# An attention layer and an FP4 feed-forward layer: weight squares in PSUM, rests of x on VectorE, attention up to three batches ahead

## The chip, the cores and the metric

The kernel runs on one core of one Trainium2 chip. The metric is the device time of one execution in microseconds (us), the median of several runs.

## The reference

`out` is x with 8 batches of T = 512 rows and D = 256 columns. An attention-like layer without softmax comes first, then a feed-forward layer whose linear maps quantise both operands to FP4 in blocks of 16:

```python
v = out @ W_write.T                                  # values
S = out[t] . out[s-1]; M = gamma**(t-1-s), s < t     # scores, decayed and causal
x = layernorm(out + out + alpha * ((S * M) @ v) @ W_read.T)
def fp4(x):                                          # blocks of 16 along the last axis
    scale = max(max(abs(block)) / 6, 1e-12)
    return nearest_of(0, .5, 1, 1.5, 2, 3, 4, 6)(abs(block) / scale) * sign(block) * scale
h = silu(fp4(x) @ fp4(w_gate).T) * (fp4(x) @ fp4(w_up).T)    # 704 columns
x = layernorm(x + fp4(h) @ fp4(w_down).T)
```

## The kernel before, in words

**Precision.** Every matmul is done as three: each operand is split into a rounded part (`_hi`, type fp32r, by ScalarE) and a rest (`_lo`, the difference, by VectorE or GpSimd), and hi*hi, hi*lo and lo*hi are added up in PSUM. `split_matmuls` issues the three terms one after the other for each slice of the contraction (its lines 1526, 1527 and 1528 are the three terms in the profile). Everything that feeds it therefore has three steps: filled, rounded (`xT_hi_ready` and so on), rest (`xT_lo_ready`).

**Weights.** The six parts of w_ffn (4 for gate and up, 2 for down, 128 x 704 each) go through the FP4 quantiser once: `w_maxima`, `w_divisors`, `w_reciprocals` (VectorE), `w_normalise` (GpSimd), `w_squares` (ScalarE), `w_magic_add` and `w_to_grid` (VectorE), `w_dequant` (GpSimd). Nine fills then transpose them: `w_transpose` and `w_subtract` (TensorE), `w_round` and `w_remainder` (ScalarE). `combine` multiplies the two attention weights into `comb`, scaled by `scale_comb` and split by `round_comb` and `rest_comb`.

**Attention of batch n.** `x_round` (ScalarE) and `x_rest` (GpSimd) split the transposed x, of which there is one buffer (`x_full`, `xT_hi`, `xT_lo`); `scores(n, j)` for 4 row tiles of 512, 384, 256 and 128 columns; `decay_scores` (VectorE, writes `pr`), `p_round`, `p_rest`; `values(n, u)`, `v_round`, `v_rest`; `reads(n, u)`; `x_residual` (z), `x_deviations`, `x_moments`, `x_rstd`, `x_layernorm` (writes `x1`, two buffers, by which batches' attention may be ahead of the feed-forward layer); then the FP4 quantiser of x (`x_maxima` to `x_dequant`), `xq_transpose`, `xq_round`, `xq_rest`.

**Feed-forward of tile k** (32 tiles of 128 rows, k = 4b + t): `gate_up(k, b, t, half)`, `gate_silu`, `hidden`, the quantiser of h (`h_maxima` to `h_dequant`), `h_repeat`, `h_transpose(k, t, g)`, `h_round`, `h_rest`, `down(k, t)`, `out_residual`, `out_deviations`, `out_moments`, `out_rstd`, `out_layernorm`, `store`.

**What sets the order.** Each of the five engine blocks (and SP's list of loads and stores) is an order written out by hand: a head, a `body(b, par)` that `run` repeats for b = 2 to 5, and a tail. An engine does its list strictly in order; each helper waits on semaphores for its inputs and for the buffers that it overwrites (`wait_ge`), and a `free` list names what frees a PSUM bank. PSUM has 8 banks: four of `gu` for gate_up, and `bank[0]` to `bank[3]`, shared by all else by the tables `v_bank`, `s_bank`, `r_bank`, `h_bank`, `d_bank`, `w_bank`. TensorE starts with 28 matmuls on zeros.

Of the kernel before, what the change touches and what calls it, by code (L numbers as in the profile page):

```python
# [30 lines left out]
F32 = mybir.dt.float32  # L31
# [6 lines left out]
P = 128  # L38
# [14 lines left out]
def mk_seq_postln_kernel(nc, x_rows, xt_rows, w_attn, w_ffn, decay, log_alpha, out):  # L53
# [12 lines left out]
    WU = 6  # L66
    LAST = B - 1
    p_at = [sum(T - P * i for i in range(j)) for j in range(TILES + 1)]

    with ExitStack() as ctx:  # L70
# [47 lines left out]
        x1 = sb("x1", [P, 2, TILES, D])  # L118
# [32 lines left out]
        o_off = sb("o_off", [P, 2, D])  # L151
# [13 lines left out]
        w_bank = (bank[0], gu[:, 3, :], bank[0], gu[:, 2, :], gu[:, 1, :], gu[:, 0, :], bank[2], bank[2], bank[0])  # L165
# [43 lines left out]

        def w_dst(w):  # L210
            return wq_gu[:, w * I:(w + 1) * I] if w < 4 else wq_dn[:, w - 4, 0:I]
# [23 lines left out]
        def run(body):  # L235

            for b in range(2, B - 2):
                body(b, b % 2)
# [5 lines left out]
        def _(sp):  # L244
# [81 lines left out]
        def _(pool):  # L326
# [1534 lines left out]
```

## Time and profile before

| | |
|---|---|
| median of 3 runs (lowest, highest) | 336.72 us (336.69, 338.21) |
| profiled execution, its own time | 336.96 us |
| its span in the trace | 335.2 us |
| TensorE matmul busy | 319.0 us, 95%, 2271 instructions |
| VectorE busy | 293.7 us, 88%, 750 |
| GpSimd busy | 250.6 us, 75%, 261 |
| ScalarE busy | 213.4 us, 64%, 516 |
| TensorE on the chain that ended last | 75% |

In the profile PE is TensorE, PEld its weight loads (they overlap the matmuls), DVE is VectorE, ACT is ScalarE, POOL is GpSimd, SP issues DMAs. Matmuls overlap, so their rate is read from start to start, not from the length of one. The granted clock is a share of 2.4 GHz; the other level is 1.2 GHz, 0.50.

### The profile page before, as it was taken

The page shows a single profiled execution, that of the slowest core. Times are in us where ns is not written, and L with a number is a line of the kernel's source. Part 1 is how long each engine was busy: PE and PEld are TensorE (multiplying, and loading weights), DVE is VectorE, ACT ScalarE, POOL GpSimd, SP SyncE. Part 2 cuts the span into 40 slices and gives each one's busy share as a digit, 9 for nine tenths or more (in the row PEclk, how much of TensorE's full clock was granted, in tenths as well). Part 3 has the DMA queues.
Part 4 walks back from the last instruction along what each step waited for, and adds up shares of the span by engine and source line. Part 5 has one row for each costly group of instructions (what it writes and reads, how often), then busy time and mean ns, then how long its engine had stood idle before and what let it go on. Part 6 is the DMA issues. An engine that isn't in the chain of part 4 may idle for free.

```text
span 335.2 us, 6881 instructions
## 1 busy us (share of the span) xinstructions
PE 319.0 (95%) x2271; PEld 305.7 (91%) x2271; DVE 293.7 (88%) x750; ACT 213.4 (64%) x516; POOL 250.6 (75%) x261
## 2 busy tenths in 40 slices
PE   8587899999999999999999999999999999999993
PEld 3376899999999999999999999999999999999983
DVE  3888789999899998989799988989989989999972
ACT  3545895775838656755847665764847656665664
POOL 1898968875887947884977857795886777876862
PEclk9989999999999999999999999999999999999999
DMA  5610300300022102200031002200002000000002
GB/s 197 261 51 12 116 3 0 125 3 3 0 80 79 33 1 80 78 18 17 3 104 71 16 2 80 80 31 2 16 3 87 8 18 18 17 19 16 32 18 79
DMA packets 8243, 15.71 MB, mean 47 GB/s; under 512 B 1168, under 2 KB 5264, under 8 KB 8208
## 3 DMA queue, kind: packets, MB, share of 16 engines
q1 hardware_dynamic: 7920, 15.27, 13.6%
q8 instruction: 18, 0.29, 0.4%
q14 instruction: 17, 0.14, 0.1%
q10 hardware_dynamic: 288, 0.00, 0.0%
HBM read 11.08 MB, written 4.19 MB: 46 GB/s over the span
## 4 chain that ended last, share of the span: by engine, by line
PE 75%; ACT 8%; DVE 6%; POOL 4%; issue 3%; DMA 2%; ACTq 0%; POOLq 0%; DVEq 0%
PE bank L1528 11%; PE bank L1526 11%; PE bank L1527 11%; PE gu L1526 11%; PE gu L1528 10%; PE gu L1527 10%; PE bank L1600 6%; PE bank L1576 2%; DMA scal<-in_log_alpha_dram 2%; DVE h_g L991 1%; POOL wq_gu L349 1%; ACT h_sq L571 1%; PE bank L1610 1%; PE bank L1611 1%; ACT x L616 1%
## 5 line engine op out<-in xcount | busy, mean ns | idle before, releaser
L1526 PE MATMUL gu<-guT_hi,xqT_hi 128*128 128x352 f32 x256 | 85.2, 333 | 0.1
L1528 PE MATMUL gu<-guT_hi,xqT_lo 128*128 128x352 f32 x256 | 82.5, 322 | 0.0
L1527 PE MATMUL gu<-guT_lo,xqT_hi 128*128 128x352 f32 x256 | 82.5, 322 | 0.0
L398 POOL TENSOR_TENSOR h_q<-h_g,h_ns 128x704 f32<-128x704 f32 x32 | 45.4, 1419 | 18.9 <-DVE h_g L991 17.7
L1526 PEld LDWEIGHTS gu<-guT_hi,xqT_hi 128*128 128x128 f32 x256 | 48.1, 188 | 0.9 <-DVE xqT_lo L1078 0.4
L1527 PEld LDWEIGHTS gu<-guT_lo,xqT_hi 128*128 128x128 f32 x256 | 48.2, 188 | 0.2
L1528 PEld LDWEIGHTS gu<-guT_hi,xqT_lo 128*128 128x128 f32 x256 | 48.1, 188 | 0.0
L391 POOL TENSOR_TENSOR h_n<-w_raw,h_rs 128x704 f32<-128x704 f32 x32 | 46.1, 1441 | 2.5 <-DVE h_rs L981 2.4
L644 ACT ACTIVATE w_raw<-gu 128x352 f32<-128x352 f32 x64 | 29.5, 461 | 28.5 <-PE gu L1528 28.1
L1528 PE MATMUL bank<-dnT_hi,hqT_lo 128*128 128x256 f32 x160 | 44.8, 280 | 0.0
L1527 PE MATMUL bank<-dnT_lo,hqT_hi 128*128 128x256 f32 x160 | 44.7, 279 | 0.0
L1526 PE MATMUL bank<-dnT_hi,hqT_hi 128*128 128x256 f32 x160 | 44.7, 279 | 0.0
L383 POOL TENSOR_TENSOR x_q<-x_g,x_ns 128x512 f32<-128x512 f32 x16 | 20.6, 1285 | 31.7 <-DVE x_g L991 31.6
L986 DVE SCALAR_TENSOR_TENSOR h_y<-h_sq,h_n 128x704 f32<-128x704 bf16 x38 | 38.0, 1000 | 3.3 <-ACT h_sq L571 1.7
L355 POOL TENSOR_TENSOR pr_lo<-pr,pr_hi 128x512 fp32r<-128x512 f32 (+3 forms) x32 | 35.5, 1112 | 1.1 <-ACT pr_hi L608 1.1
L665 ACT CAST hqT_hi<-bank 128x512 fp32r<-128x512 f32 x64 | 29.7, 472 | 8.6 <-PE bank L1600 8.6
L991 DVE SCALAR_TENSOR_TENSOR h_g<-h_sq,h_y 128x704 f32<-128x704 bf16 x38 | 35.0, 927 | 0.2
L1115 DVE TENSOR_TENSOR hqT_lo<-bank,hqT_hi 128x512 fp32r<-128x512 f32 x64 | 34.0, 544 | 0.5 <-ACT hqT_hi L665 0.4
L1087 DVE TENSOR_TENSOR w_raw<-w_raw,gu 128x352 f32<-128x352 f32 x64 | 32.2, 502 | 1.8 <-ACT w_raw L644 1.6
L1600 PE MATMUL bank<-ident,h_q 128*128 128x128 f32 x192 | 28.8, 273 | 1.7 <-DVE hqT_lo L1115 1.1
L1527 PEld LDWEIGHTS bank<-dnT_lo,hqT_hi 128*128 128x128 f32 x160 | 30.0, 188 | 0.0
L1528 PEld LDWEIGHTS bank<-dnT_hi,hqT_lo 128*128 128x128 f32 x160 | 30.0, 188 | 0.0
(123 smaller groups left out, 937.4 us busy)
## 6 DMA issues: line engine op xcount, KB each, us to landing
x_full<-in_xt_rows_dram SPq DMA_DIRECT2D x8, 512.0 KB, 3.6
xs<-in_x_rows_dram SPq DMA_DIRECT2D x8, 512.0 KB, 3.3
out_dram<-wq_gu SPq DMA_DIRECT2D x32, 128.0 KB, 1.7
w_raw<-in_w_ffn_dram SPq DMA_DIRECT2D x6, 352.0 KB, 7.9
w_pair<-in_w_attn_dram SPq DMA_DIRECT2D x1, 512.0 KB, 7.4
scal<-in_decay_dram ACTq DMA_DIRECT2D x1, 0.5 KB, 3.0
scal<-in_log_alpha_dram ACTq DMA_DIRECT2D x1, 0.5 KB, 5.1
```

The lines of the kernel that those rows point to most:

```text
L355: nc.gpsimd.tensor_tensor(pr_lo[:, c], pr[:, c], pr_hi[:, c].bitcast(F32), ALU.subtract).then_inc(pr_lo_ready, 1)
L391: nc.gpsimd.tensor_tensor(blocks(h_n[:, p, :]), blocks(h[:, p, :]), per_block(h_rs[:, p, :], HB), ALU.mult).then_inc(h_norm, 1)
L398: nc.gpsimd.tensor_tensor(blocks(h_q[:, p, 0:I]), blocks(h_g[:, p, :]), per_block(h_ns[:, p, :], HB), ALU.mult).then_inc(h_quant, 1)
L665: nc.scalar.copy(hqT_hi[:, t % 2, c], h_bank[t][g][:, 0:c.stop - c.start]).then_inc(hT_hi_ready, 1)
L986: nc.vector.scalar_tensor_tensor(y, sq, MAGIC_C, v, ALU.add, ALU.add).then_inc(magic_sem, 1)
L991: nc.vector.scalar_tensor_tensor(g, sq, MAGIC_C, y, ALU.add, ALU.subtract).then_inc(grid_sem, 1)
L1087: nc.vector.tensor_tensor(h[:, p, c], silu[:, p, c], gu[:, 2 * half + 1, 0:HALF], ALU.mult).then_inc(h_ready, 1)
L1115: nc.vector.tensor_tensor(hqT_lo[:, p, c], h_bank[t][g][:, 0:c.stop - c.start], hqT_hi[:, p, c].bitcast(F32), ALU.subtract).then_inc(hT_lo ...
L1526: nc.tensor.matmul(dst, lh, rh, start=(first and i == 0), stop=False)
L1527: nc.tensor.matmul(dst, lh, rl, start=False, stop=False)
L1528: last = nc.tensor.matmul(dst, ll, rh, start=False, stop=(i == len(terms) - 1))
L1600: last = nc.tensor.transpose(h_bank[t][g][:, at - h_part[g].start:at - h_part[g].start + P], h_q[:, t % 2, at:at + P], ident[:])
```

## The change

- `w_squares` of the four gate and up parts write float32 into two banks of `gu` (one buffer for all four) instead of a bfloat16 tile in SBUF; the warming matmuls use `gu[:, 3]`.
- `x_rest` of batches 0 and 1 is done by VectorE, of the others still by GpSimd.
- z and x1 share one tile with four buffers (`XBUF = 4`) and layer norm works in place; `z_off` and `o_off` become bfloat16 (they are written and never read).
- TensorE's groups wait for the rounded parts first; the terms with the rests come last, behind the waits for them (`split_matmuls` with `rests`, new `late_matmuls`). In `down` the last term moves to the end.
- PSUM banks are dealt anew, and the order of all engines is written anew: `body` now covers b = 2 to 4, scores of batch b + 3 are issued in the body of b. The number of instructions of each other kind stays.

```diff
+    XBUF = 4
-        z = sb("z", [P, TILES, D])
-        z_off = sb("z_off", [P, TILES, D])
+        z_off = sb("z_off", [P, TILES, D], BF16)
-        x1 = sb("x1", [P, 2, TILES, D])
+        x1 = sb("x1", [P, XBUF, TILES, D])
-        v_bank, xq_bank = (bank[2], bank[1]), (bank[1], bank[2])
-        s_bank, r_bank = (bank[1], bank[3], bank[3], bank[3]), (bank[2], bank[0])
-        h_bank = ((bank[1], bank[2]), (bank[0], bank[1]), (bank[0], bank[3]), (bank[0], bank[2]))
-        d_bank = (bank[2], bank[1], bank[3], bank[0])
+        v_bank, xq_bank = (bank[2], bank[1]), (bank[0], bank[2])
+        s_bank, r_bank = (bank[1], bank[3], bank[0], bank[3]), (bank[2], bank[3])
+        h_bank = ((bank[1], bank[0]), (bank[1], bank[0]), (bank[0], bank[2]), (bank[0], bank[2]))
+        d_bank = (bank[3], bank[1], bank[3], bank[2])
...
+        def w_sq(w):
+            return gu[:, 0:2, 0:HALF] if w < 4 else halves(h_sq[:, w % 2, :])
...
             load_x_transposed(2)
             load_x(1)
+            load_x_transposed(3)
             load_x(2)
-            load_x_transposed(3)
-            store(0, 0)
             load_x_transposed(4)
             load_x(3)
+            load_x_transposed(5)
+            store(0, 0)
...
             def w_squares(w):
                 act.wait_ge(w_norm, w + 1)
-                nc.scalar.activation(h_sq[:, w % 2, :], h_n[:, w % 2, :], ACT.Square,
-                                     scale=ROOT_K).then_inc(w_square, 1)
+                if 1 <= w < 4:
+                    act.wait_ge(w_grid, w)
+                nc.scalar.activation(w_sq(w), halves(h_n[:, w % 2, :]), ACT.Square, scale=ROOT_K).then_inc(w_square, 1)
...
             w_magic_add(0)
+            x_rest(0, 0)
+            x_rest(0, 1)
+            w_to_grid(0)
+            scale_comb()
+            w_maxima(2)
+            dve.wait_ge(mask_ready, 1)
+            decay_scores(0, 0)
+            w_divisors(2)
+            decay_scores(0, 1)
+            rest_comb()
             w_magic_add(1)
-            w_maxima(2)
-            w_to_grid(0)
+            decay_scores(0, 2)
+            decay_scores(0, 3)
             w_to_grid(1)
-            scale_comb()
-            w_divisors(2)
             w_reciprocals(2)
+            v_rest(0, 0)
...
-            def split_matmuls(dst, terms, first=True):
+            def split_matmuls(dst, terms, rests, first=True, end=True):
 
                 for i, (lh, ll, rh, rl) in enumerate(terms):
                     nc.tensor.matmul(dst, lh, rh, start=(first and i == 0), stop=False)
                     nc.tensor.matmul(dst, lh, rl, start=False, stop=False)
+                wait_all(rests)
+                for i, (lh, ll, rh, rl) in enumerate(terms):
+                    last = nc.tensor.matmul(dst, ll, rh, start=False, stop=(end and i == len(terms) - 1))
+                return last
+
+            def late_matmuls(dst, terms, rests):
+
+                for i, (lh, ll, rh, rl) in enumerate(terms):
+                    nc.tensor.matmul(dst, lh, rh, start=(i == 0), stop=False)
+                wait_all(rests)
+                for i, (lh, ll, rh, rl) in enumerate(terms):
+                    nc.tensor.matmul(dst, lh, rl, start=False, stop=False)
                     last = nc.tensor.matmul(dst, ll, rh, start=False, stop=(i == len(terms) - 1))
                 return last
...
             combine([])
             scores(0, 0, [])
-            scores(0, 1, [])
-            w_transpose(0, [])
-            w_transpose(1, [])
-            pe.wait_ge(comb_lo_ready, 1)
-            values(0, 0, [(comb_ready, 1)])
-            scores(0, 2, [(pr_ready, 2)])
-            values(0, 1, [(pr_ready, 1)])
-            w_subtract(0)
-            scores(0, 3, [(pr_ready, 3)])
-            reads(0, 0, [(v_lo_ready, 1)])
-            reads(0, 1, [(wT_lo_ready, 1)])
+            scores(0, 1, [(comb_ready, 1)])
+            scores(0, 2, [])
+            scores(0, 3, [(pr_ready, 2)])
+            pe.wait_ge(comb_lo_ready, 1)
+            values(0, 0, [])
+            values(0, 1, [(pr_ready, 1)])
+            reads(0, 0, [(v_lo_ready, 1)])
+            w_transpose(0, [(pr_ready, 3)])
+            reads(0, 1, [(pr_ready, 4)])
+            w_subtract(0)
...
+                gate_up(k + 1, b, 1, 1)
+                reads(n + 1, 0, [(v_lo_ready, 2 * n + 3)])
+                down(k - 3, 1, [(hT_lo_ready, 2 * k - 5)])
+                xq_transpose(n - 1, 1, [(z_ready, 2 * n + 3)])
+                h_transpose(k - 2, 2, 0, [(hT_lo_ready, 2 * k - 4)])
+                scores(n + 1, 3, [(o_ready, 4 * n - 7)])
+                values(n + 1, 1, [(o_ready, 4 * n - 6)])
+                gate_up(k + 2, b, 2, 0)
+                h_transpose(k - 2, 2, 1, [(xqT_lo_ready, 2 * n)])
+                gate_up(k + 2, b, 2, 1)
+                h_transpose(k - 1, 3, 0, [(hT_lo_ready, 2 * k - 3)])
+                h_transpose(k - 1, 3, 1, [(hT_lo_ready, 2 * k - 2)])
+                down(k - 2, 2, [(pr_ready, k + 12)])
+                scores(n + 2, 0, [(v_lo_ready, 2 * n + 4)])
             run(body)
```

## Rows read from the trace of the kernel before

**Rows 1.** Busy us (instructions) of the engines by stretch; granted clock, DMA.

```profile
0.00:42.00 42.00, 32.91 (x184) 24.72 (x185) 30.49 (x67) 22.81 (x46) 31.80 (x34) 0.96 0.36 127
42.00:95.00 53.00, 52.83 (x373) 51.31 (x372) 49.54 (x117) 38.57 (x90) 40.59 (x39) 1.00 0.07 24
95.00:250.00 155.00, 155.00 (x1136) 153.02 (x1135) 140.32 (x372) 98.59 (x249) 119.21 (x125) 1.00 0.13 42
...
sum 335.20, PE 319.02 PEld 305.66 DVE 293.68 ACT 213.41 POOL 250.61; mean PE 63.80 PEld 61.13 DVE 58.74 ACT 42.68 POOL 50.12
```

**Rows 2.** TensorE's waits to 90 us: for whom, total, times, longest.

```profile
PE bank L1526 <- POOL xT_lo L360: 3.4, 1, 3.4
PE bank L1526 <- DVE pr L1022: 2.0, 3, 1.1
...
PE bank L1526 <- POOL pr_lo L355: 1.1, 1, 1.1
PE bank L1623 <- POOL wq_gu L349: 0.6, 1, 0.6
PE bank L1631 <- ACT guT_hi L577: 0.5, 1, 0.5
```

**Rows 3.** TensorE's waits from 40 us to the end.

```profile
PE bank L1600 <- DVE hqT_lo L1115: 1.1, 2, 0.6
PE bank L1600 <- DVE wq_gu L1124: 0.6, 1, 0.6
PE bank L1526 <- DVE pr L1022: 0.3, 1, 0.3
```

**Rows 4.** TensorE in windows of 1 us: length, busy, granted clock, DMA.

```profile
16.00:17.00 1.00, 1.00 (x5) 0.59 0.73 176
...
18.00:19.00 1.00, 1.00 (x5) 0.50 0.04 16
```

**Rows 5.** Timeline of TensorE: start, us, instruction.

```profile
9.95 1.97 PE L1640 MATMUL bank<-w_pair 128*128 128x256 f32 x8 [0.18 <-DMA w_pair<-in_w_attn_dram]
...
134.42 0.40 PE L1526 MATMUL bank<-xT_hi 128*128 128x512 f32 x1
...
135.81 0.32 PE L1526 MATMUL gu<-guT_hi,xqT_hi 128*128 128x352 f32 x1
...
137.74 0.34 PE L1526 MATMUL bank<-xT_hi 128*128 128x384 f32 x1
```

**Rows 6.** Chain that ended last, in order of time: start, us, what.

```profile
123.39 0.44 PE bank L1576 x4
...
160.63 0.44 PE bank L1576 x4
```

**Rows 7.** VectorE's instructions by form: count, busy us, mean ns, idle before.

```profile
L986 DVE SCALAR_TENSOR_TENSOR h_y<-h_sq,h_n 128x704 f32<-128x704 bf16 x38 | 38.0, 1000 | 3.3 <-ACT h_sq L571 1.7 <-ACT h_sq L649 1.6
L991 DVE SCALAR_TENSOR_TENSOR h_g<-h_sq,h_y 128x704 f32<-128x704 bf16 x38 | 35.0, 927 | 0.2
...
L1028 DVE TENSOR_TENSOR v_lo<-bank,v_hi 128x512 fp32r<-128x512 f32 x16 | 10.9, 683 | 2.8 <-ACT v_hi L601 2.5
...
L1022 DVE TENSOR_TENSOR pr<-bank,mask 128x512 f32<-128x512 f32 x8 | 5.2, 650 | 0.2 <-issue 0.2
...
L1143 DVE TENSOR_TENSOR comb_lo<-comb,comb_hi 128x512 fp32r<-128x512 f32 x1 | 1.0, 1001 | 0.0
L1138 DVE TENSOR_SCALAR comb<-bank,scal 128x512 f32<-128x512 f32 x1 | 0.7, 737 | 0.0
```

**Rows 8.** Timeline of the other engines ahead of the first scores.

```profile
10.83 1.12 ACT L594 CAST xT_hi<-x_full 128x512 fp32r<-128x512 f32 x2
...
10.96 1.50 DVE L986 SCALAR_TENSOR_TENSOR h_y<-h_sq,h_n 128x704 f32<-128x704 bf16 x1 [0.71 <-ACT h_sq L571]
...
11.67 3.61 POOL L360 TENSOR_TENSOR xT_lo<-x_full,xT_hi 128x512 fp32r<-128x512 f32 x2
```

**Rows 9.** Timeline of TensorE, its last matmul.

```profile
329.83 0.28 PE L1528 MATMUL bank<-dnT_hi,hqT_lo 128*128 128x256 f32 x1
```

More of the change, by code:

```diff
@@ L1239, in _ @@
+            h_magic_add(0, 0)
+            x_residual(2, 0)
+            v_rest(2, 1)
+            x_maxima(1, 1)
+            x_magic_add(1, 0)
+            x_to_grid(1, 0)
+            h_maxima(2, 0)
+            h_magic_add(1, 1)
+            hidden(3, 1, 0)
+            x_residual(2, 1)
+            h_to_grid(0, 0)
+            x_moments(2, 0)
+            decay_scores(3, 0)
+            x_divisors(1, 1)
+            hidden(3, 1, 1)
+            xq_rest(1, 0)
             h_divisors(2, 0)
+            h_reciprocals(2, 0)
@@ new lines, in _ @@
+            h_rest(14, 2, 1)
+            h_divisors(17, 1)
+            x_maxima(5, 1)
+            v_rest(6, 1)
+            h_reciprocals(17, 1)
+            x_divisors(5, 1)
+            hidden(18, 0, 0)
+            hidden(18, 0, 1)
+            x_reciprocals(5, 1)
+            h_to_grid(16, 0)
+            out_residual(14, 2)
+            h_rest(15, 3, 0)
+            h_magic_add(17, 1)
+            x_moments(6, 0)
+            h_maxima(18, 0)
+            hidden(19, 1, 0)
+            decay_scores(7, 0)
@@ L1374, in _ @@
[L1374 to L1384 removed]
+            v_rest(7, 1)
+            xq_rest(6, 0)
+            hidden(23, 1, 0)
+            x_divisors(7, 0)
+            out_residual(18, 2)
+            h_magic_add(21, 1)
@@ new lines, in _ @@
+            gate_up(4, 1, 0, 0)
+            h_transpose(0, 0, 1, [(xqT_lo_ready, 3)])
+            gate_up(4, 1, 0, 1)
+            values(3, 0, [(wT_lo_ready, 9)])
+            h_transpose(1, 1, 0, [(hT_lo_ready, 1)])
+            pe.wait_ge(wT_lo_ready, FILLS)
+            down(0, 0, [(pr_ready, 14)])
+            scores(3, 2, [(hT_lo_ready, 2)])
+            gate_up(5, 1, 1, 0)
+            h_transpose(1, 1, 1, [(pr_ready, 15)])
+            gate_up(5, 1, 1, 1)
+            reads(3, 0, [(v_lo_ready, 7)])
@@ new lines, in _ @@
+            down(1, 1, [(hT_lo_ready, 3)])
+            xq_transpose(1, 1, [(z_ready, 7)])
+            scores(3, 3, [(o_ready, 1)])
+            values(3, 1, [(o_ready, 2)])
+            h_transpose(2, 2, 0, [(hT_lo_ready, 4)])
+            gate_up(6, 1, 2, 0)
+            h_transpose(2, 2, 1, [(xqT_lo_ready, 4)])
+            gate_up(6, 1, 2, 1)
+            down(2, 2, [(pr_ready, 16)])
+            scores(4, 0, [(v_lo_ready, 8)])
+            h_transpose(3, 3, 0, [(hT_lo_ready, 5)])
+            h_transpose(3, 3, 1, [(hT_lo_ready, 6)])
@@ new lines, in body @@
+                scores(n + 2, 0, [(v_lo_ready, 2 * n + 4)])
+            run(body)
+            gate_up(19, 4, 3, 0)
+            gate_up(19, 4, 3, 1)
+            scores(7, 1, [(o_ready, 15)])
+            h_transpose(16, 0, 0, [(pr_ready, 29)])
+            scores(7, 2, [(hT_lo_ready, 31)])
+            down(15, 3, [(hT_lo_ready, 32)])
+            h_transpose(16, 0, 1, [(pr_ready, 31)])
+            reads(6, 1, [(pr_ready, 30)])
+            values(7, 0, [(o_ready, 16)])
+            xq_transpose(5, 0, [(hT_lo_ready, 34)])
@@ new lines, in _ @@
+            h_transpose(17, 1, 0, [(hT_lo_ready, 33)])
+            down(16, 0, [(z_ready, 14)])
+            gate_up(20, 5, 0, 0)
+            gate_up(20, 5, 0, 1)
+            reads(7, 0, [(v_lo_ready, 15)])
+            h_transpose(17, 1, 1, [(xqT_lo_ready, 11)])
+            gate_up(21, 5, 1, 0)
+            down(17, 1, [(hT_lo_ready, 35)])
+            h_transpose(18, 2, 0, [(hT_lo_ready, 36)])
+            xq_transpose(5, 1, [(z_ready, 15)])
+            gate_up(21, 5, 1, 1)
+            scores(7, 3, [(o_ready, 17)])
```

1519 lines of the change are left out of this document (799 added, 720 removed).

## The prediction

> **What bounds the kernel now.** I read four views in this order. First the windows by stretch: from 42 us on TensorE is busy all but 0.17 us of 53, and from 95 to 250 us all of 155, while VectorE has 49.5 of 53 and 140.3 of 155 [rows 1]. The chain that ended last says the same: it runs through TensorE alone there, and the same piece comes back after 37.24 us in the next batch [rows 6]. Second, I asked whether "busy" hides idle matmuls. The timeline gives start to start: six 512-column matmuls take 1.39 us (0.232 each), twelve of 352 take 1.93 us (0.161 each) [rows 5]. The other forms, read in the same way, are 0.174 (384 columns), 0.119 (256), 0.112 (128) and 0.11 for a transpose. A batch has 24 score matmuls (6 of each width: 3.8 us), 24 of values (2.9), 30 of reads (3.6), 96 of gate_up (15.5), 68 of down (8.1) and 32 transposes (3.5): 37.4 us, the 37.24 of the chain within 0.5%. So a batch is a full queue of matmuls at their own rate, and no order of it can be shorter. Waits between groups cost nothing visible there.
>
> What remains is time in which TensorE has no matmul or runs slowly. That is the third view, its waits. At the head it loses 3.4 us for xT_lo, 2.0 for pr, 1.1 for pr_lo, 0.6 for the first quantised weights and 0.5 for guT_hi: 7.6 us [rows 2]. After the longest of these its granted clock fell to 0.59 in 16 to 17 us and 0.50, its 1.2 GHz level, in 18 to 19 us [rows 4]; the scores of 15.3 to 19.3 us lose 0.41 + 0.50 + 0.50 and a little, 1.5 us. From 40 us to the end it loses 1.1 + 0.6 + 0.3 = 2.0 us [rows 3]. Together 11.1 us. Before the first (combine ends at 9.95 + 1.97 = 11.92 [rows 5]) DMA and warming are untouched, and behind the last matmul, at 329.83 + 0.28 = 330.1 [rows 9], the last output tile's chain takes the other 5.1 us of the span of 335.2.
>
> **The change part by part.** No matmul is added or removed, so all turns on these 11.1 us.
>
> *Rests of x on VectorE.* GpSimd's two subtractions took 3.61 us, beginning at 11.67 [rows 8]. On VectorE they stand behind magic_add of weight part 0, which begins at 10.96 as before. That instruction took 1.50 us [rows 8]; with its square in PSUM I take 0.93, the mean of h_g (0.927), between 0.8 and 1.50. For one x_rest the trace has two neighbours of the same width: v_lo with one PSUM operand, 0.683, and comb_lo with both operands in SBUF, 1.001 [rows 7]. I take 0.9, since its operands are comb_lo's but GpSimd is partly idle. So xT_lo is ready at 10.96 + 0.93 + 1.8 = 13.7 us (bounds 13.1 and 14.5), not 15.3.
>
> The row on comb_lo is also where a rule of the Trainium skill speaks against this change: GPSIMD Engine Reference, section Specifications, says that GpSimd's SBUF interfaces are shared with VectorE and contend with VectorE instructions that have two SBUF inputs. By it four x_rests at comb_lo's price would cost 4.0 us and by v_lo's 2.7, and GpSimd's own work beside them would stretch; the trace agrees in direction (1.001 against 0.683).
>
> *Products with the high parts first.* scores(0,0) no longer waits for xT_lo but for xT_hi, ready at 10.83 + 1.12 = 11.95 [rows 8]. It does 0.47 us of its 1.39, then waits from 12.4 to 13.7: **1.3 us** in place of 3.4. It ends at 14.6. The new waits inside a group cost nothing where they are already met, as the waits between groups now do.
>
> *The new order at the head.* comb now sits in bank 3, where scores(0,1) goes too, so that this waits for scale_comb: VectorE does to_grid (0.93) and comb (0.74 [rows 7]) and is done at 15.4: **0.8 us**. scores(0,1) and (0,2) take 1.04 + 0.71, to 17.1. scores(0,3) needs decay_scores(0,1), which stands behind a maxima, decay_scores(0,0) (0.65) and two small ones: about 17.5, **0.4 us**. values(0,0) needs comb_lo, 1.0 us further: **0.2 us**. Then 24 matmuls of values, 2.9 us, to 21.4; reads(0,0) needs v_lo of values(0,0), behind magic_add(1), two decays, to_grid(1), a reciprocal and v_rest: 18.5 + 0.93 + 0.7 + 0.93 + 0.4 + 0.6 = 22.0, **0.4 us** once overlaps are taken off. Walked on like this, scores(1,1) waits **0.4** for x_residual(0,1) (its bank), w_transpose(2) **0.1** for a decay, and I find no other wait until gate_up(0), which starts near 43 us with two groups of scores of batch 2 already done. Sum 3.6 us (bounds 1.8 and 6) against 7.6. Moving x_full's next loads behind VectorE's x_rests makes them earlier; stores wait behind load_x_transposed(5) on SP, but no store is waited for until its slot is used a batch later.
>
> *Clock.* TensorE's idle is now in pieces of 1.3, 0.8 and 0.4 us with work between, not one of 3.4. I take 0.5 us of loss, between nothing and the 1.5 of now. The Trainium skill, TensorE: Matmul & The Clock Gate, section Part 1, has the clock follow how busy the array has been; by it the fall could come again here and the sum would be 1.0 us worse.
>
> *Squares of weights in PSUM.* ScalarE's w_squares(1 to 3) now wait for the grid before (one buffer). Behind the first stand round_comb and p_round; its grid is done at 14.6, comb itself at 15.4, so it delays nothing. VectorE gains at most 4 x 0.57 = 2.3 us of contended time, which pays for part of the 3.6 us of four x_rests.
>
> *Attention ahead, four buffers.* Counted in TensorE's own work, tile k's transposes now come 26 to 31 us behind its gate_up where they came 22 to 26 us, and a batch's xq_transpose 51 to 63 us behind its reads where it was 16 to 26. For the last tile it is 10.1 us where it was 7.6. So more work lies ready at each wait of [rows 3], which paid 2.0 us. I take 0.9: the last tile's own chain through silu, hidden, maxima, normalise, square, grid and dequantisation is about as long as the 10.1 us that now lie beside it (0.4), and VectorE is dense in between (0.5). BF16 in place of F32 for the squared deviations, which nobody reads, and layer norm in place, cost nothing: same elements on ScalarE.
>
> **Sum.** 11.1 lost now; 3.6 + 0.5 + 0.9 = 5.0 after. That is 6.1 us less than the profiled execution's own 336.96 us: 330.9. The median shown is 336.72, 0.24 lower, so I predict **330.7 us**. Own range 328.8 to 332.8.
>
> **Rivals.** *A, VectorE takes over from 42 to 95 us.* It has 3.5 us free of 53 there now [rows 1]. With the form view's means laid on the new list (checked on the old: 295 us against 293.68 [rows 1]), VectorE's work ahead of the third down is 82.7 us against TensorE's 81.4; before, 71.8 against 69.3. VectorE starts 3.1 us before TensorE's combine and TensorE waits 3.6 at the head, so VectorE may idle 5.4 us until then. Each us beyond is lost: with 8 idle, as now (of 15.0 us that it is not busy up to 95 us [rows 1], some 6 lie ahead of its first instruction on a weight part and 1 behind the third down), 2.6 us, so 333.3. For it: the head's VectorE work is denser. Against: now its work leads by more (40.0 against 35.2 at the third tile's gate_up, after 41.2 against 41.8), and TensorE did not wait.
>
> *B, nothing to measure.* A and a full clock loss and the head at its bound of 6 us: 2.6 + 1.0 + 2.4 of the 6.1 are gone, 336.7.
>
> *C, slower: x's single buffer.* scores of batch n+2 start only 6.8 us of TensorE's work behind values(n+1,1), which frees xT_hi (9 us now). In between ScalarE rounds twice, once behind a silu, and GpSimd's x_rests (up to 3.61 us [rows 8]) follow an out_rstd that waits for VectorE. I count 2.2 us to spare. If GpSimd is later than that by L, each of batches 4 to 7 pays L; from L = 1.9 us (four times 1.5 is the whole gain, and the 0.4 per batch that is needed for slower by 0.5%) it decides: at L = 2 us, 8 us, 338.7. For it: GpSimd's list is in order. Against: that order has its out_rstd ahead of the need by a tile.
>
> *D, better than forecast.* Head 1.8 us, clock kept, nothing later: 11.1 - 1.8 = 9.3 less, 327.4.
>
> **Chances.** Forecast 0.60, A 0.20, B 0.07, C 0.07, D 0.06. A measurement of this kernel can tell about 0.5% from no change: below 335.0 is faster, above 338.4 slower. Forecast, A and D are faster: 0.86. B is the same: 0.07. C is slower: 0.07. The range leaves out B, C and the ends of D and A: 328.0 to 335.0.
>
> **What would show it.** In the profile after: TensorE's wait for xT_lo near 1.3 us and at VectorE; a sum of its waits before 45 us near 3.6; granted clock mostly 1.00 from 15 to 20 us; gate_up(0) near 43 us; a batch still repeating after 37.2 us; x_rest on VectorE near 0.9 us and magic_add(0) near 0.93. It is wrong if a wait for xT_lo shows once per batch (C), if VectorE is busy without a gap and TensorE waits for it between 42 and 95 us (A), or if the matmuls' rates differ when the low parts come last, which no row here shows.

## The result and the profile after

The changed kernel takes **328.31 us** (median of 4 runs, 328.27 to 328.37) against 336.71 (336.68 to 338.21, 4 runs): a ratio of 0.9748, interval 0.9736 to 0.9760. The forecast was 330.7 with a range of 328.0 to 335.0. The profiled execution took 328.27 us, 8.69 less than the 336.96 of the one before. One execution of u_squares, below, ran at a granted clock of 0.56 from end to end and took 521.68 us against 332.27 to 332.98 in its others; no run here shows why, its ratio leaves that one out, and its profile is the one of a further run.

First the windows by stretch of the kernel after (length, busy us and instructions of each engine, granted clock, DMA share, GB/s), which answer to [rows 1]:

```profile
0.00:42.00 42.00, 39.55 (x240) 31.23 (x241) 35.15 (x92) 29.13 (x60) 29.21 (x35) 1.00 0.41 142
42.00:95.00 53.00, 52.38 (x377) 51.40 (x376) 49.35 (x114) 37.15 (x87) 42.32 (x39) 1.00 0.09 30
95.00:250.00 155.00, 154.72 (x1140) 152.94 (x1139) 138.79 (x371) 98.59 (x252) 118.51 (x128) 1.00 0.12 39
```

In the first 42 us TensorE has 240 matmul instructions where it had 184. The other stretches are as full as they were, within half a microsecond. So the time comes out of the head, as it had to.

TensorE's waits to 90 us, and then from 40 us to the end (for whom; total, times, longest). They answer to [rows 2] and [rows 3]; the wait of the warming for its zeros is left out, as before, and the one for h_q of ScalarE is at 81.7 us and stands in both lists:

```profile
PE bank L1696 <- DVE xT_lo L1096: 0.7, 1, 0.7
PE bank L1771 <- ACT h_q L687: 0.6, 1, 0.6
PE bank L1693 <- DVE comb L1225: 0.4, 1, 0.4
...
PE bank L1771 <- POOL h_q L406: 0.4, 1, 0.4
PE bank L1683 <- DVE wq_gu L1211: 0.3, 1, 0.3
```

Waits of the head: 0.7 + 0.4 = 1.1 us where there were 7.6. Waits from 40 us on: 0.6 + 0.4 + 0.3 = 1.3 where there were 2.0. Windows of 1 us show the granted clock where it had been 0.59 and 0.50 [rows 4]:

```profile
16.00:17.00 1.00, 0.94 (x8) 0.77 (x7) 1.00 (x5) 0.86 (x2) 0.22 (x1) 1.00 0.00 0
...
18.00:19.00 1.00, 1.00 (x11) 1.00 (x10) 1.00 (x4) 0.41 (x1) 1.00 (x2) 1.00 0.00 0
```

It is 1.00 (2.4 GHz), here and in every window from 11 to 25 us. By the prediction's own bookkeeping TensorE now loses 1.1 + 0 + 1.3 = 2.4 us where it lost 11.1. That is 8.7 less, and the profiled execution is 8.69 shorter. That the two agree to the hundredth is luck: the lists leave out pieces of 0.2 us and less, and the bookkeeping takes a batch as unchanged, which it is not quite (below). The part behind the last matmul did not change: it ends at 321.18 + 0.28, 5.0 us ahead of the end of the span of 326.5, against 5.1.

The timeline of TensorE: the first scores, the steady state and the last matmul (start, us, instruction), as in [rows 5] and [rows 9]:

```profile
9.98 1.89 PE L1812 MATMUL bank<-w_pair 128*128 128x256 f32 x8
11.84 0.72 PE L1693 MATMUL bank<-xT_hi 128*128 128x512 f32 x2
13.26 0.50 PE L1696 MATMUL bank<-xT_lo,xT_hi 128*128 128x512 f32 x1 [0.70 <-DVE xT_lo L1096]
...
124.12 0.60 PE L1745 MATMUL bank<-ident,x_q 128*128 128x128 f32 x4
...
161.25 0.60 PE L1745 MATMUL bank<-ident,x_q 128*128 128x128 f32 x4
...
321.18 0.28 PE L1785 MATMUL bank<-dnT_hi,hqT_lo 128*128 128x256 f32 x1
```

The two products of the high parts run at 11.84, beside the end of x_rest, and the first product with a rest follows at 13.26. A batch repeats after 161.25 - 124.12 = 37.13 us, against 37.24 [rows 6]. gate_up(0) starts at 41.39 us, where the forecast had near 43.

The timeline of VectorE in the same stretch, which answers to [rows 8]:

```profile
10.75 0.89 DVE L1063 SCALAR_TENSOR_TENSOR h_y<-gu,h_n 128x704 f32<-128x704 f32 x1 [0.73 <-ACT gu L601]
11.56 1.64 DVE L1096 TENSOR_TENSOR xT_lo<-x_full,xT_hi 128x512 fp32r<-128x512 f32 x2
13.12 0.88 DVE L1068 SCALAR_TENSOR_TENSOR h_g<-gu,h_y 128x704 f32<-128x704 f32 x1
13.93 0.73 DVE L1225 TENSOR_SCALAR comb<-bank,scal 128x512 f32<-128x512 f32 x1
...
16.65 0.67 DVE L1230 TENSOR_TENSOR comb_lo<-comb,comb_hi 128x512 fp32r<-128x512 f32 x1
```

magic_add(0) took 0.89 us (1.50 before), each x_rest 0.82, comb_lo 0.67 (1.00 before [rows 7]).

### The profile page after: what moved, and what is told of

Read it like the earlier page. It is cut to its first block, busy times and chain, and to the rows that moved or that the text cites. A ratio compares the mean times of both kernels' runs of the same rounds, so it can differ in the third digit from the quotient of the medians.

```text
span 326.5 us, 6927 instructions
## 1 busy us (share of the span) xinstructions
PE 317.1 (97%) x2271; PEld 304.1 (93%) x2271; DVE 291.2 (89%) x754; ACT 211.8 (65%) x516; POOL 241.2 (74%) x257
## 4 chain that ended last, share of the span: by engine, by line
PE 69%; DVE 14%; ACT 6%; issue 5%; POOL 3%; DMA 2%; ACTq 0%; DVEq 0%; POOLq 0%
PE gu L1683 9%; PE gu L1687 9%; PE gu L1684 9%; PE bank L1683 6%; PE bank L1684 6%; PE bank L1687 6%; PE bank L1693 5%; PE bank L1697 5%; PE bank L1696 5%; PE bank L1771 5%; DVE h_g L1068 2%; DVE h_y L1063 2%; DVE w_raw L1174 2%; DVE hqT_lo L1202 2%; DMA scal<-in_log_alpha_dram 2%
## 5 line engine op out<-in xcount | busy, mean ns | idle before, releaser
L406 POOL TENSOR_TENSOR h_q<-h_g,h_ns 128x704 f32<-128x704 f32 x32 | 49.2, 1537 | 38.9 <-DVE h_g L1068 36.7
L1687 PE MATMUL gu<-guT_hi,xqT_lo 128*128 128x352 f32 x256 | 61.7, 322 | 0.0
L1687 PEld LDWEIGHTS gu<-guT_hi,xqT_lo 128*128 128x128 f32 x256 | 44.5, 188 | 0.0
L1684 PE MATMUL bank<-dnT_lo,hqT_hi 128*128 128x256 f32 x160 | 39.1, 279 | 0.0
L1683 PE MATMUL bank<-dnT_hi,hqT_hi 128*128 128x256 f32 x160 | 39.1, 279 | 0.0
L1063 DVE SCALAR_TENSOR_TENSOR h_y<-h_sq,h_n 128x704 f32<-128x704 bf16 x34 | 34.5, 1013 | 3.8 <-ACT h_sq L678 3.6
L1068 DVE SCALAR_TENSOR_TENSOR h_g<-h_sq,h_y 128x704 f32<-128x704 bf16 x34 | 30.7, 904 | 0.0
L1683 PEld LDWEIGHTS bank<-dnT_hi,hqT_hi 128*128 128x128 f32 x160 | 30.1, 188 | 0.0
L706 ACT ACTIVATE wq_gu<-wq_gu,o_shift,o_rstd 128x256 f32<-128x256 f32 x32 | 19.2, 602 | 16.3 <-POOL o_shift L415 16.3
L1181 DVE TENSOR_REDUCE h_am<-w_raw 128x44 f32<-128x704 f32 x32 | 28.0, 876 | 0.3
```

Of the source, the lines that this page charges most:

```text
L406: nc.gpsimd.tensor_tensor(blocks(h_q[:, p, 0:I]), blocks(h_g[:, p, :]), per_block(h_ns[:, p, :], HB), ALU.mult).then_inc(h_quant, 1)
L1063: nc.vector.scalar_tensor_tensor(y, sq, MAGIC_C, v, ALU.add, ALU.add).then_inc(magic_sem, 1)
L1068: nc.vector.scalar_tensor_tensor(g, sq, MAGIC_C, y, ALU.add, ALU.subtract).then_inc(grid_sem, 1)
L1683: nc.tensor.matmul(dst, lh, rh, start=(first and i == 0), stop=False)
L1684: nc.tensor.matmul(dst, lh, rl, start=False, stop=False)
L1687: last = nc.tensor.matmul(dst, ll, rh, start=False, stop=(end and i == len(terms) - 1))
```

## The experiments

In the expectations theory 1 is the prediction's account: each part takes its own piece of TensorE's lost time away, at the prices of the prediction. Theory 2 is the rival that each of them states. Each kernel was timed beside the kernel before, which gave 336.71 to 336.79 in every batch of runs. "After" is the changed kernel, "before" the one before.

### Undoing one part

**u_squares**: the squares of the gate and up parts go to the bfloat16 tile in SBUF again.

```diff
         def w_sq(w):
-            return gu[:, 0:2, 0:HALF] if w < 4 else halves(h_sq[:, w % 2, :])
+            return halves(h_sq[:, w % 2, :])
...
-                if 1 <= w < 4:
-                    act.wait_ge(w_grid, w)
+                if w >= 2:
+                    act.wait_ge(w_grid, w - 1)
```

The second half goes with two buffers in place of one: ScalarE may square a part one grid earlier.

> The changed kernel with one part undone: squares of all weight parts go to the bfloat16 tile in SBUF again. If the PSUM squares paid by keeping VectorE and GpSimd apart (theory 1), magic_add and to_grid of the four parts lengthen again from 0.89 where GpSimd works beside them, the first one to between 1.0 and 1.5 us, and the time rises by 0.8 us (0.3 to 1.5), to 329.1. If all of the 2.3 us that the prediction gave them lay on the path (theory 2), it rises to 330.6. If VectorE had cover at the head (rival), it stays at 328.3.

Measured: 332.98 us (ratio 0.9880, interval 0.9863 to 0.9896), **4.7 us** over after and outside both theories.

**u_squares_look**: the same kernel, once, with its profile.

> The same kernel as u_squares, for its waits, since that one's profiled execution ran at half clock. Theory 1: the 4.5 us are a chain: magic_add(0) beside GpSimd takes up to 1.5 us, and xT_lo, comb and the first decays shift behind it, each a wait of TensorE; waits before 45 us sum to 4 us or more, with VectorE's magic_add and to_grid of the weights at 1.1 us or more each. Theory 2, the granted clock falls at the head again and half of the 4.5 us is clock. Theory 3, the squares' time itself is the same and the two-buffer order on ScalarE is what costs.

332.92 us, 4.6 over after. VectorE and GpSimd of this kernel in the head, on the timeline:

```profile
10.85 1.46 DVE L1063 SCALAR_TENSOR_TENSOR h_y<-h_sq,h_n 128x704 f32<-128x704 bf16 x1 [0.75 <-ACT h_sq L601]
12.23 1.70 DVE L1096 TENSOR_TENSOR xT_lo<-x_full,xT_hi 128x512 fp32r<-128x512 f32 x2
...
17.92 1.42 DVE L1230 TENSOR_TENSOR comb_lo<-comb,comb_hi 128x512 fp32r<-128x512 f32 x1
19.26 1.70 DVE L1063 SCALAR_TENSOR_TENSOR h_y<-h_sq,h_n 128x704 f32<-128x704 bf16 x1
...
10.18 1.39 POOL L350 TENSOR_TENSOR h_n<-w_raw,h_rs 128x704 f32<-128x704 f32 x1 [0.18 <-DVE h_rs L1058]
11.52 1.26 POOL L345 TENSOR_SCALAR_AFFINE_SELECT mask<-mask 128x512 f32<-128x512 f32 x1
```

h_y takes 1.46 us in place of 0.89, all behind it is 0.6 to 0.7 us later, and comb_lo, which now starts while GpSimd is at pr_lo, takes 1.42 in place of 0.67. Behind it h_y of the second part takes 1.70 in place of 0.88, and h_g of the third and fourth 1.55 and 1.78 in place of 0.89 and 0.87. TensorE's waits of this kernel and its clock in windows of 1 us (here TensorE alone: busy, granted clock, DMA share, GB/s):

```profile
PE bank L1696 <- DVE xT_lo L1096: 1.4, 1, 1.4
PE bank L1693 <- ACT v_hi L630: 0.7, 1, 0.7
PE bank L1795 <- DVE pr L1104: 0.7, 1, 0.7
```

```profile
16.00:17.00 1.00, 1.00 (x5) 0.50 0.48 193
...
19.00:20.00 1.00, 1.00 (x9) 0.80 0.00 0
```

The shares are read from the starts of the same matmuls in both kernels. At scores(0,1) TensorE is 0.7 us behind after (15.54 against 14.81), at values(0,0) 2.0 (19.55 against 17.57), at reads(0,0) 2.6 (23.32 against 20.69), at the first transposes of x's quantised pair 4.7 (44.45 against 39.76), and so it stays to the end. The first step is h_y of part 0. The second, 1.25 us, is the clock at its 1.2 GHz level for three windows (16 to 19 us) and at 0.80 in a fourth. The third is the wait for v_hi, behind comb_lo and the second h_y, and the last 2 us go with waits for decays (pr) that stand behind the two slow h_g. One of the four executions of u_squares had a mean granted clock of 1.00 and took 332.27 us, so without a fall of the clock 4.0 us of the loss are still there (that execution has no trace). The expectation had put the whole edit at 0.8 us. So the squares in PSUM are worth more than the 3.0 us that their eight instructions take longer, because each step that comes late also decides what the next ones run beside. The other buffering on ScalarE shows no cost at the first scores: the square of part 1 came at 11.75 us in place of 14.10, and ScalarE then idled for 2.9 us.

**u_pool**: x_rest of batches 0 and 1 goes back to GpSimd, in its places of before.

```diff
             w_normalise(1)
+            x_rest(0, 0)
+            x_rest(0, 1)
             mask_pairs()
...
             w_magic_add(0)
-            x_rest(0, 0)
-            x_rest(0, 1)
```

> The changed kernel with x_rest of batches 0 and 1 on GpSimd again, at its old places. Theory 1, the move of x_rest is the largest part of the gain: xT_lo is ready at 14.5 us or later instead of 13.2, TensorE waits 2 us there, the granted clock falls again behind it, and with batch 1's the time rises by 2 to 4 us, to 331.3. Rival, the high-parts-first order already covers the wait: it rises by 0.7 us at most.

Measured: 331.05 us (0.9838, 0.9822 to 0.9855), **2.7 us** over after. TensorE's waits, GpSimd and VectorE:

```profile
PE bank L1693 <- DVE x L1130: 1.7, 1, 1.7
...
PE bank L1696 <- POOL xT_lo L366: 1.2, 1, 1.2
PE bank L1683 <- DVE comb_lo L1234: 0.8, 1, 0.8
```

```profile
25.27 1.39 POOL L350 TENSOR_TENSOR h_n<-w_raw,h_rs 128x704 f32<-128x704 f32 x1
...
27.48 0.89 DVE L1067 SCALAR_TENSOR_TENSOR h_y<-gu,h_n 128x704 f32<-128x704 f32 x1 [2.08 <-ACT gu L605]
```

3.7 us against 1.1, which is 2.6, and the clock stays 1.00. The time is theory 1's, its account is not. The longer wait for xT_lo costs nothing: scores(0,1) starts at 14.85 against 14.81, since VectorE, free of the x_rests, has comb ready earlier and the wait for comb is gone. What costs is comb_lo, which starts 0.03 us behind GpSimd's pr_lo and takes 1.79 us, and most of all the rests of batch 1. On GpSimd these stand ahead of h_n of weight part 2, which comes at 25.27 instead of 21.93. VectorE waits 2.1 us for its square, and x_residual(0,1), next in VectorE's list, is what TensorE waits 1.7 us for.

**u_waits**: TensorE's groups wait for the rests before their first product; the order of the products is after's.

```diff
             def late_matmuls(dst, terms, rests):
 
+                wait_all(rests)
                 for i, (lh, ll, rh, rl) in enumerate(terms):
                     nc.tensor.matmul(dst, lh, rh, start=(i == 0), stop=False)
-                wait_all(rests)
...
                 pe.wait_ge(hT_hi_ready, 2 * k + 2)
+                pe.wait_ge(hT_lo_ready, 2 * k + 2)
```

`split_matmuls` has the same edit as `late_matmuls`; the last two lines are in `down`.

> The changed kernel with its order of matmuls, but every group waits for the rests before its first matmul. Theory 1: only the first scores group gains by it, 0.47 us, and one or two groups of the head a little; the time rises by 0.7 us (0.4 to 1.2), to 329.0, and the wait for xT_lo shows 1.2 us instead of 0.7. Rival, the late waits matter in every batch: it rises by over 2 us and waits show once per batch.

Measured: 330.28 us (0.9807, 0.9792 to 0.9821), **2.0 us** over after, between the two theories. Its second group of scores, and its transposes of x's quantised pair in two batches, on the timeline (after has 14.81, 124.12 and 161.25):

```profile
14.90 0.55 PE L1694 MATMUL bank<-xT_hi 128*128 128x384 f32 x2
...
125.88 0.60 PE L1745 MATMUL bank<-ident,x_q 128*128 128x128 f32 x4
...
163.18 0.60 PE L1745 MATMUL bank<-ident,x_q 128*128 128x128 f32 x4
```

At the first scores the early high parts give nothing: the wait for xT_lo is 1.7 us in place of 0.7, but scores(0,1) starts only 0.09 us later, because in after TensorE then waits for comb. By the first transposes of the quantised pair u_waits is 0.7 us behind (40.42 against 39.76). gate_up(0) adds a wait of 0.4 for xqT_lo. By the batches' transposes the lag is 1.2 (88.16 against 86.99), 1.76, 1.93 and 2.1 (200.48 against 198.39), and 1.9 at the last one (291.86 against 289.97). So of the 2.0 us some 1.2 are lost by gate_up(0) and the rest by 200 us; a batch takes 163.18 - 125.88 = 37.30 us and not 37.13, but the 0.17 do not go on adding up in the later ones. I had put the whole at 0.7.

**u_all**: all three undone, which leaves the new order (that of the products inside a group too), banks and buffers.

> The changed kernel with the three parts undone together (squares in SBUF, x_rest of batches 0 and 1 on GpSimd, waits for the rests first): what is left of the change is its order, its banks and the four buffers. If the parts add up (4.5 + 2.7 + 2.0), it takes 337.5 us and the order alone is worth nothing. If they overlap, because each alone was hidden by another, it takes 332 to 335 us and the order brings the rest. If the order is itself worse without them, over 338.

Measured: 338.59 us (1.0047, 1.0030 to 1.0064), **1.9 us slower than before**. Its longest wait:

```profile
PE bank L1694 <- POOL xT_lo L366: 3.5, 1, 3.5
```

9.1 of the 10.3 us between it and after are lost in the head (its first transposes of x's quantised pair come at 48.82, after's at 39.76), the rest in the batches. By after's 1.1 that makes 10.2 us lost in the head, where before loses 7.6 + 1.5 = 9.1. The new order alone is no gain; 10.3 us of after's lead over this kernel is the three parts on top of it. Undone one at a time they cost 4.7 + 2.7 + 2.0 = 9.4, undone together 10.3: nearly additive once the order is there.

### One part, or the three parts, on the kernel before

**b_rest**: before, with x_rest(0) alone moved to VectorE.

```diff
             w_magic_add(0)
+            x_rest(0, 0)
+            x_rest(0, 1)
             w_magic_add(1)
```

> The kernel before with one part alone: x_rest of batch 0 on VectorE behind magic_add(0), nothing else moved. Theory 1: xT_lo is ready near 14.2 us instead of 15.3, the wait of 3.4 us shrinks to 2.3, and the later chain of comb and weight part 1 on VectorE moves back by as much as VectorE does more (1.6 us), so 0 to 1.5 us are won (1 more if the clock stays up): 335.7. Rival, the move alone brings most of the 8.4 us: below 332. Other side: it delays comb and the first decays and the kernel gets slower, 337.5.

Measured: 336.77 us (0.9999, 0.9990 to 1.0009), **nothing**. Its two longest waits:

```profile
PE bank L1628 <- POOL wq_gu L349: 3.6, 1, 3.6
PE bank L1531 <- DVE xT_lo L1017: 1.4, 1, 1.4
```

The wait for xT_lo fell from 3.4 [rows 2] to 1.4 us, and a wait of 3.6 us for the first quantised weights stands where one of 0.6 was: the order of before asks for them right behind scores(0, 1), and TensorE, freed earlier, only gets to them earlier.

**b_parts**: before's order with all three parts (squares of three weight parts in PSUM, rests of batches 0 and 1 on VectorE, high parts first).

> The kernel before, in its own order and with its banks, with the three parts put in: squares of weight parts 0 to 2 in PSUM (part 3 stays in SBUF), x_rest of batches 0 and 1 on VectorE, high parts first. If the parts alone bring the gain, it takes 329 to 331 us. If they need the new order of VectorE and TensorE at the head, the waits move on as in b_rest and it takes 333 to 336.5 us.

Measured: 334.69 us (0.9943, 0.9928 to 0.9958), **2.0 us** less than before. The same wait is there, and the clock falls behind it (windows of 1 us, TensorE alone):

```profile
PE bank L1650 <- POOL wq_gu L355: 3.5, 1, 3.5
```

```profile
18.00:19.00 1.00, 0.32 (x2) 0.50 0.00 0
...
23.00:24.00 1.00, 1.00 (x6) 0.50 0.00 0
```

So neither half does it: the order alone +1.9 us, the parts alone -2.0, both -8.4 (the halves meet only nearly, since part 3's square stays in SBUF here). The parts bring the first operands earlier; the order gives TensorE something to do (all scores, the values and the first reads) until the weights come.

**b_head**: b_parts with a new order of the first 40 us as well, written by me after the pattern of after: scores(0, 2), values and scores(0, 3) ahead of the transposes of weights, w_subtract(0) behind reads(0, 0).

```diff
             scores(0, 1, [])
-            w_transpose(0, [])
-            w_transpose(1, [])
+            scores(0, 2, [(pr_ready, 2)])
...
+            w_transpose(0, [])
+            w_transpose(1, [])
             reads(0, 0, [(v_lo_ready, 1)])
+            w_subtract(0)
```

> The kernel before with the three parts (squares of weight parts 0 to 2 in PSUM, rests of x of batches 0 and 1 on VectorE, high parts first) and now a new order of the first 40 us alone: TensorE takes scores(0, 2), the values and scores(0, 3) ahead of w_transpose(0) and (1), and w_subtract(0) behind reads(0, 0), with VectorE, ScalarE and GpSimd to match. The body, the tail, the two x1 buffers and attention's lead of the kernel before stay. Theory 1 (the new order is worth what it saves in the head, since the wait for the quantised weights at the first transposes goes, 3.5 us, and the lost clock behind it): 330.5 to 331.5 us, with the late waits of the body (2.0 us) left. Theory 2 (the attention's lead and the four buffers are needed for it, or the wait only moves to the next use of the weights): 334 us or more.

Measured: 339.30 us (1.0070, 1.0049 to 1.0091), 4.6 us **slower** than b_parts. Its waits, and ScalarE on its timeline:

```profile
PE bank L1658 <- ACT guT_hi L580: 4.9, 1, 4.9
...
PE bank L1650 <- POOL wq_gu L355: 1.1, 1, 1.1
```

```profile
23.75 0.76 ACT L575 ACTIVATE gu<-h_n 128x704 f32<-128x704 f32 x1 [2.43 <-POOL h_n L350]
...
28.64 0.30 ACT L611 CAST pr_hi<-pr 128x128 fp32r<-128x128 f32 x1 [2.75 <-DVE pr L1030]
28.84 0.58 ACT L580 CAST guT_hi<-bank 128x512 fp32r<-128x512 f32 x1
```

The wait for wq_gu did fall, from 3.5 to 1.1 us. But in my order ScalarE has w_squares(2) and (3) ahead of w_round(0); GpSimd reaches their inputs only at 23.7 and 25.1 us, VectorE's decay for p_round stands behind them too, and w_round(0) comes at 28.84 with TensorE idle for 4.9 us. This is a fault of my order and says nothing on whether the lead of the attention and the four buffers are needed. That stays open.

### Versions meant to be better

**v_head**: after, with x_round and x_rest(0) ahead of the first weight part's square and magic_add, scale_comb ahead of both of its steps, round_comb ahead of w_squares(1), and the first decays ahead of w_maxima(2).

> The changed kernel with its first 16 us reordered: ScalarE rounds x before it squares weight part 0, VectorE does x_rest(0) and scale_comb before magic_add(0), and the first decays before the maxima of weight part 2. TensorE's waits of 0.7, 0.4 and 0.2 us before 17 us go. If TensorE's head is what sets the time, 327.2 us; if VectorE, which is busy without a gap from 11 to 42 us, only passes the wait on to reads(0,0), 328.3; if weights come late by it, up to 329.5.

Measured: 329.42 us (0.9782, 0.9768 to 0.9797), **1.1 us slower** than after. VectorE and GpSimd on its timeline:

```profile
10.61 2.60 DVE L1096 TENSOR_TENSOR xT_lo<-x_full,xT_hi 128x512 fp32r<-128x512 f32 x2 [0.44 <-ACT xT_hi L623]
...
10.25 1.39 POOL L350 TENSOR_TENSOR h_n<-w_raw,h_rs 128x704 f32<-128x704 f32 x1 [0.24 <-DVE h_rs L1058]
```

The pair of x_rests starts 0.95 us earlier than in after and ends at the same 13.2: it takes 2.60 us in place of 1.64. The weights are later (h_g of part 1 at 20.05 us, against 18.58), v_rest stands behind them, and TensorE waits 1.2 us for v_lo.

**after_again**: after once more, on the chip of the next two (and of b_head).

> The changed kernel itself once more, on the chip of the three that follow, so that differences of a few tenths of a microsecond can be read. All theories: 328.3 us, 0.975 of the kernel before; on another figure the three that follow are to be read against that.

Measured: 328.36 us (0.9745, 0.9727 to 0.9762).

**v_tail**: after, with the two late waits for h_q aimed at.

```diff
+            v_round(3, 0)
+            h_repeat(1, 1)
             out_deviations(0, 0)
-            v_round(3, 0)
             x_squares(1, 1)
-            h_repeat(1, 1)
...
-            out_residual(26, 2)
             h_maxima(31, 1)
             h_divisors(31, 1)
+            h_reciprocals(31, 1)
+            out_residual(26, 2)
             h_rest(28, 0, 0)
-            h_reciprocals(31, 1)
```

> The changed kernel with two late waits aimed at: on ScalarE v_round(3, 0) and h_repeat(1, 1) go ahead of out_deviations(0, 0) (TensorE waited 0.6 us for h_q at 81.7 us), and on VectorE in the last stretch h's maxima, divisors and reciprocals of tile 31 go ahead of out_residual(26) and h_rest(28, 0, 0) (0.4 us for h_q at 315.9 us). Theory 1 (each late wait of TensorE is paid in full at the end): both go, 327.3 us. Theory 2 (the wait moves to whatever was put behind, or the last tile's chain has another link): 328.3 us, the same as before this edit.

Measured: 328.84 us (0.9758, 0.9740 to 0.9775), 0.5 us over after. Its waits from 40 us to the end:

```profile
PE bank L1771 <- DVE hqT_lo L1202: 0.9, 2, 0.6
PE bank L1771 <- POOL h_q L406: 0.4, 1, 0.4
```

The wait of 0.6 us at 81.7 us is gone, and paid out: the transposes at 198.39 us in after come at 197.99. The edit in the tail lost more than that: the 0.4 for the last tile's h_q did not move, and h_rest, now later, holds TensorE twice for 0.9 us. Each theory was right for one half. By these starts I estimate about 327.9 us for an order with the first edit alone; it was not run.

**v_comb**: v_tail, and scale_comb ahead of w_to_grid(0), round_comb ahead of w_squares(1).

> The same as the one with both late waits aimed at, and besides VectorE scales comb ahead of w_to_grid(0) and ScalarE rounds it ahead of w_squares(1), so that the wait for comb in the head (0.4 us) should go. Theory 1 (TensorE's first products are what bounds the head): 0.3 to 0.4 us less than that one. Theory 2 (the two are only traded for weights that come later, or for work that falls beside GpSimd's and takes longer, as in the run where the first 16 us were reordered): the same or up to 1 us more.

Measured: 331.22 us (0.9811, 0.9787 to 0.9836), **2.4 us over v_tail**. VectorE and GpSimd on its timeline, and TensorE's windows of 1 us:

```profile
17.00 1.75 DVE L1230 TENSOR_TENSOR comb_lo<-comb,comb_hi 128x512 fp32r<-128x512 f32 x1
18.68 0.88 DVE L1063 SCALAR_TENSOR_TENSOR h_y<-gu,h_n 128x704 f32<-128x704 f32 x1
...
16.93 1.27 POOL L361 TENSOR_TENSOR pr_lo<-pr,pr_hi 128x512 fp32r<-128x512 f32 x1 [0.64 <-ACT pr_hi L637]
```

```profile
19.00:20.00 1.00, 1.00 (x5) 0.50 0.00 0
```

comb is ready 0.6 us earlier, and the wait of 0.4 for it is gone. But comb_lo now starts 0.07 us behind GpSimd's pr_lo, where in after it starts 0.13 us ahead of it (16.65 against 16.78), and takes 1.75 us in place of 0.67. magic_add(1) starts 1.4 us later. TensorE waits 0.9 for pr and 0.7 for comb_lo, and behind these its clock is at 0.50 from 19 to 22 us. Not in every execution: of the five, two took 329.87 and 330.01 us at a mean granted clock of 0.998 and 0.999, three 331.22 to 331.51 at 0.990 to 0.994. So some 1.1 us over v_tail are the order's, and the other 1.3 or so come and go with the clock. None of the three versions beats after.

## Why the prediction was right, and where it was off

**The bound.** Right in the main. TensorE's queue of matmuls sets the body, and nearly all of the change lies in the 11.1 us of lost time: 11.1 - 2.4 = 8.7 against 8.69 measured. "No order of it can be shorter" was too strong: a batch takes 37.13 us and not 37.24.

**The sum was mis-sized: 5.0 us forecast as lost, 2.4 found.** By its terms:

| | before | forecast | measured |
|---|---|---|---|
| waits of the head | 7.6 | 3.6 | 1.1 |
| clock | 1.5 | 0.5 | 0 |
| late waits | 2.0 | 0.9 | 1.3 |

**Head.** The forecast walk gave 1.3 for xT_lo and 0.8 for comb; the list has 0.7 and 0.4. VectorE was priced too high at nearly every step: magic_add(0) 0.93 (0.89), x_rest 0.9 (0.82), to_grid 0.93 (0.88), comb_lo 1.0 (0.67), with magic_add starting at 10.75 and not 10.96 (which is not the change's doing: in b_rest it starts at 10.75 too). These leave comb at 14.66, not 15.4, and the smaller waits behind it (0.4, 0.2, 0.4, 0.4, 0.1) then do not open; what is left of them are gaps of 0.2 us at most from start to start.

**Clock.** It stayed at 1.00, and the 0.5 us forecast for it were not lost. That this had to be so is not shown. With idle pieces of 0.7 and 0.4 us (after) it stays, with 1.4 and 0.4 ahead of 16 us (u_squares_look) it falls to 0.50 for three windows, with 0.8, 0.9 and 0.7 (v_comb) for three as well, and behind one piece of 3.5 us (b_parts) for six. The Trainium skill, TensorE: Matmul & The Clock Gate, section Part 1, has the clock follow how busy the array was; these four runs agree in direction. Three others do not fall in line: it stays at 1.00 with 1.7 in one piece (u_waits), with 1.2, 0.8 and 1.7 (u_pool) and with 0.7, 0.6 and 1.2 (v_head). And the executions of v_comb differ among themselves. The idle time listed here does not say alone whether the clock falls.

**Squares in PSUM.** Here the prediction's bound was too narrow: "VectorE gains at most 4 x 0.57 = 2.3 us", which "pays for part of" the x_rests. Undone, the part cost 4.7 us of the kernel. The gain on the instructions is already over the bound (h_y and h_g together take 72.2 us in after and 75.2 in u_squares_look, and comb_lo 0.67 against 1.42). The larger error is that the bound counted busy time only: 0.7 us of it lies on the chain xT_lo, comb, decay, and the later ones hold the decays and v_rest, for which TensorE waits.

**Rests on VectorE.** xT_lo came at 13.2 us, 0.5 ahead of the forecast, and the move is worth 2.7 us in after's order. But it is not worth them where the prediction put them, at the first wait for xT_lo: u_pool loses nothing there, 0.8 at comb_lo and 1.9 at the x_residual behind weight part 2. Nothing of the prediction prices what the rests of batch 1 do to GpSimd's list. That u_pool's total met its expectation is luck. The rule of the Trainium skill, GPSIMD Engine Reference, section Specifications, that the prediction held against the move, contention of GpSimd with VectorE instructions with two SBUF inputs, is seen here too, at a small price. The first pair took 1.64 us and the second 1.37, where a pair with GpSimd idle takes 1.28 (b_rest, b_parts). v_head shows what it costs in a worse slot (2.60).

**High parts first.** The two products do run ahead of the wait at the first scores, but that is worth 0.09 us, since TensorE then waits for comb. "The new waits inside a group cost nothing" held. That the same edit would save 1.9 us elsewhere, 1.2 of them by gate_up(0) and the rest in the batches up to 200 us, was not seen, since the argument took a batch of 37.24 us for a full queue that can't be shorter. The rates did not change with the low parts last.

**Attention ahead, four buffers.** 1.3 us of late waits against 0.9. They are others than before: h_q at 81.7 us, whose h_repeat stands behind an out_deviations on ScalarE, and the last tile's own chain, which took 0.4 as forecast. Whether the greater lead took the old ones away (1.1 for hqT_lo, 0.6 for wq_gu) was not tried by itself.

**The rivals.** *A*: VectorE has 3.65 us free of 53 from 42 to 95 us, and no wait there is for VectorE's feed-forward work. Not seen. *B*: not seen. *C*: no wait for xT_lo after the first, and a batch repeats after 37.13 us. Not seen. *D* (head 1.8, clock kept, nothing later, 327.4) was nearest: head and clock went its way, the late waits did not. The result lies between D and the forecast, and a chance of 0.06 for D was too small.

**What stays open.** What the lead of the attention and the four buffers are worth alone; b_head was to tell, and a fault of its own hid it. The new banks and the bfloat16 z_off and o_off were not tried by themselves. And why the clock falls with one pattern of idle pieces and not with another.

## What to carry to other kernels

When a chain of waits binds the start, undo and redo its parts together with the order: here the order alone lost 1.9 us, the parts alone won 2.0, both won 8.4, and one part alone (b_rest) won nothing because the wait moved to the next operand. Price a step of VectorE by what GpSimd is doing at the moment when it starts, not by its mean; put one of its operands in PSUM where it is on the chain. And when a wait goes, look at when the next group starts: the longer wait for xT_lo in u_pool and u_waits cost under 0.1 us, because the wait for comb behind it took it up, and the price stood at other groups.

## What the runs showed of the hardware

**VectorE's instructions with two SBUF operands wait for the end of GpSimd's, within a few hundredths.** comb_lo alone takes 0.67 us (after). In v_comb it starts at 17.00 under a pr_lo that ends at 16.93 + 1.27 = 18.20, and ends at 18.75, 0.55 later; in u_squares_look it starts at 17.92, pr_lo (17.52, 1.27 us) ends at 18.79, and it ends at 19.34, again 0.55 later. Before's comb_lo, the 1.00 us that the forecast took as a price [rows 7], is such a case too: it ran from 19.55 to 20.55 under a dequantisation of GpSimd that ended at 20.01. The first x_rest behaves the same: with 0.55 us from the end of GpSimd's mask select and 0.6 for the second of the pair, the pair should end at 12.05 + 1.15 = 13.20 in after (13.20 is seen), at 13.93 in u_squares_look (13.93) and at 13.36 in v_comb (13.36). In v_head the two engines take turns: h_n ends at 11.64, the first x_rest goes, then the select (11.59 + 1.07 = 12.66), then the second, which ends at 13.21. GpSimd waits in the same way: the select takes 0.61 us in after and 1.26 in u_squares_look, where h_y stands in its way until 12.31. And h_y with its square in PSUM, started at 10.75 under a running h_n, takes 0.89 as if alone; with the square in SBUF it ends 0.74 us behind h_n's end.

The Trainium skill, SBUF — State Buffer, section SBUF: two separate sides, says just this: the pair of ports that the two engines share goes wholly to whichever instruction starts first, and VectorE asks for it only with two SBUF inputs (or in a mode with two ports). The trace agrees, with the ends above. By it the forecast's 0.93 for magic_add(0), taken between 0.8 and 1.50, lay between two cases of which only one can happen. And it points at one edit that was not tried: with after's mask select out of the way of the first x_rest the pair would take 0.36 us less, by an estimate from 1.64 us here and 1.28 in b_rest.
